# A four-batch decoder on one core: from two stages in flight to three, and experts in pairs

## The reference

```python
x = _layernorm(x + _L0_attn_ref(x, ...))            # linear attention, 16 heads, decay
x = _layernorm(x + _L0_xattn_ref(x, ctx_512, ...))  # similarity, norm, softmax
x = _layernorm(x + _L0_ffn_ref(x, ...))             # gated FFN of 688 with 8 low-rank experts
x = _layernorm(x + _L1_attn_ref(x, ...))            # Mamba: 512 channels, 16 states
x = _layernorm(x + _L1_xattn_ref(x, ctx, ctx))      # softmax attention, 32 query and 8 key heads
x = _layernorm(x + _L1_ffn_ref(x, ...))             # 16 experts of 176, top 4, and one of 704

# inside _L1_attn_ref, the state h of 512 x 16 per token:
h = h * dA_t + dBu_t
y = jnp.einsum('bdn,bn->bd', h, C_t)
```

## Time and profile before

| | us |
|---|---|
| median of 3 runs | 955.67 |
| lowest, highest | 949.19, 959.2 |
| the profiled execution, its own time | 949.86 |
| span of the profiled execution | 947.7 |
| PE, DVE, ACT, POOL busy in it | 828.1, 631.5, 369.4, 358.1 |

### The profile page before, as it was taken

The page is one execution under the profiler, slowest core; times in us unless marked ns, Lnnn a source line. Parts: engine busy times, 40 slices in busy tenths (PEclk is TensorE's granted clock), DMA queues, the critical chain, the costliest instruction groups (busy, mean ns, idle before and its releaser), DMA issues.

```text
span 947.7 us, 12835 instructions
## 1 busy us (share of the span) xinstructions
PE 828.1 (87%) x4575; PEld 629.4 (66%) x4600; DVE 631.5 (67%) x1322; ACT 369.4 (39%) x796; POOL 358.1 (38%) x390
## 2 busy tenths in 40 slices
PE   6897656989999898889999997889999898679997
PEld 5675445753788786753788786753788786426886
DVE  5242699785456999884456999895456999764333
ACT  5121555327325444326324444327324444253110
POOL 4302396121034875220034976121034976000322
PEclk9998757999999999998999999999999999999999
DMA  7202400011026340311016340311024340300442
GB/s 224 102 12 82 154 36 0 1 56 60 1 63 226 118 131 0 112 67 50 1 55 232 117 129 6 111 48 68 1 57 150 117 134 0 111 2 1 145 155 78
DMA packets 26930, 76.13 MB, mean 80 GB/s; under 512 B 3436, under 2 KB 5420, under 8 KB 26228
## 3 DMA queue, kind: packets, MB, share of 16 engines
q1 hardware_dynamic: 26612, 75.26, 24.2%
q10 hardware_dynamic: 256, 0.07, 0.0%
HBM read 74.13 MB, written 1.11 MB: 79 GB/s over the span
## 4 chain that ended last, share of the span: by engine, by line
PE 53%; DVE 24%; issue 10%; POOL 7%; ACT 4%; DMA 1%; ACTq 0%; DVEq 0%; POOLq 0%; SPq 0%
PE B L806 26%; PE F L806 19%; DVE arena L1477 7%; POOL arena L493 3%; PE B L1107 3%; DVE arena L1489 3%; DVE nmx L1549 2%; PE F L835 1%; DVE q_t L1610 1%; ACT big L773 1%; DVE arena L1310 1%; POOL arena L567 1%; PE F L817 1%; DVE q_t L1615 1%; POOL rs L473 1%
## 5 line engine op out<-in xcount | busy, mean ns | idle before, releaser
L806 PE MATMUL B<-spare,mw 128*128 128x256 f32 x880 | 210.5, 383 | 6.3 <-DVE q_t L1615 5.1
L806 PEld LDWEIGHTS B<-spare,mw 128*128 128x128 f32 x880 | 164.6, 191 | 31.7 <-issue 8.5
L1477 DVE TENSOR_TENSOR_SCAN arena<-F,arena 128x512 f32<-128x512 f32 x128 | 148.8, 1206 | 1.6 <-ACT F L733 1.5
L584 POOL TENSOR_TENSOR spare<-q_t 128x256 f32<-128x256 f32 x112 | 80.7, 729 | 173.2 <-DVE q_t L1615 160.4
L493 POOL TENSOR_TENSOR arena<-du,arena 128x1024 f32<-128x1024 f32 x60 | 140.9, 2363 | 12.9 <-PE B L888 12.9
L733 ACT ACTIVATE F<-delta,a_neg 128x255 f32<-128x255 f32 x256 | 109.7, 467 | 58.2 <-DVE arena L1477 58.2
L806 PE MATMUL B<-mw,spare 128*128 128x256 f32 x448 | 117.6, 388 | 0.0
L795 ACT ACTIVATE q_t<-B 128x256 f32<-128x256 f32 x112 | 41.9, 380 | 149.9 <-PE B L806 149.8
L806 PEld LDWEIGHTS B<-mw,spare 128*128 128x128 f32 x448 | 86.5, 195 | 14.1 <-issue 1.6
L773 ACT ACTIVATE big<-B 128x512 f32<-128x512 f32 x128 | 69.4, 594 | 51.1 <-PE B L806 38.5
L1610 DVE SCALAR_TENSOR_TENSOR q_t<-q_t,B 128x256 f32<-128x256 f32 x112 | 46.6, 416 | 57.3 <-ACT q_t L795 57.0
(11 more groups left out here) (246 smaller groups left out, 1323.8 us busy)
## 6 DMA issues: line engine op xcount, KB each, us to landing
mw<-in_w_moe SPq DMA_DIRECT2D x112, 384.0 KB, 3.1
room<-in_w_f SPq DMA_DIRECT2D x4, 2544.0 KB, 9.2
arena<-b_out SPq DMA_DIRECT2D x32, 256.0 KB, 5.3
room<-in_w_l SPq DMA_DIRECT2D x4, 768.0 KB, 6.9
w_m<-in_w_m SPq DMA_DIRECT2D x1, 2112.0 KB
room<-in_w_l SPq DMA_DIRECT2D x4, 512.0 KB, 5.0
x_t<-in_x_t SPq DMA_DIRECT2D x4, 256.0 KB, 3.7
x_tok<-in_x_tok SPq DMA_DIRECT2D x4, 256.0 KB, 6.6
```

What stands on the lines that cost most here:

```text
L584: g.tensor_tensor(hid1[0:r, m % HID_RING, :], hraw[0:r, m % 3, :], crs[0:r, int(m >= MTE), :], ALU.mult)\
L806: return t_.matmul(dst, lhsT, rhs, start=start, stop=stop, skip_group_check=True)
L1477: v.tensor_tensor_scan(h, F[i][:, :], h, 0.0, ALU.mult, ALU.add)\
```

## The change

It does four things.

**Three stages.** The front is cut behind `m1` into `FRONT_A` (attention, similarity, FFN) and `FRONT_B` (Mamba). `plan(engine)` writes: front half A of batch 0 alone; A of batch 1 with B of batch 0 put between its phases (`FILL`); twice an iteration of A of batch b+1, B of batch b and the back of batch b-1 (`LATER[0]`, `LATER[1]`); B of batch 3 with the back of batch 2 (`LATER[2]`); the back of batch 3. Inside an iteration `m2` and `m3` now stand between the last phases of the FFN of the next batch.

**Places.** Batch 1's half A runs on the banks K and in a second working area. That area, `late`, is the same memory that the backs use for expert weights, queries and probabilities, so back 0 waits for `x3` of batch 1. For batches 0 and 3 (`alone`) the factors of the scan go to an SBUF tile `factors` in place of F[0] and F[1], and F[1] takes the sum that lay in K[2]. Two copies of `xa` and `xp` exist. The keys of the next back are prepared by POOL in phase `br1` of the back before.

**Batch 0's scan** has the same form as the others: halves are added on POOL, and all multiplications by C are on DVE.

**Experts in pairs.** Two units share a gate bank and an up bank: one tanh, two DVE operations and one POOL operation of 128 x 512 in place of two each of 128 x 256. The matmuls are the same.

```diff
+FRONT_A = ["load", "qkv"] + PAIRS + ["oa", "ob", "xa", "xb", "xc", "xd", "fa1", "fa2", "fa3"] + FFN_G + ["fd1", "fd2", "fd3", "m1"]
+FRONT_B = ["m2", "m3", "m4", "m5", "d1", "d2", "d3", "d4"] + STEPS + ["u1", "u2"]
+FRONT = FRONT_A[:-3] + ["m2", "fd2", "fd3", "m3", "m1"] + FRONT_B[2:]
...
+def plan(engine):
+
+    out = [("F", ph, 0) for ph in FRONT_A]
+    out += merged(FILL[engine], [("F", ph, 1) for ph in FRONT_A], [("F", ph, 0) for ph in FRONT_B])
+    back = iter([("B", ph, b) for b in range(B) for ph in (BACK if b < B - 1 else BACK_LAST)])
+    parts = [[("F", ph, b + 1 if ph in FRONT_A else b) for ph in FRONT] for b in range(1, B - 1)]
+    parts.append([("F", ph, B - 1) for ph in FRONT_B])
+    for part, after in zip(parts, LATER[engine]):
+        for item in part:
+            out += [item] + [next(back) for _ in range(after.get(item[1], 0))]
+    return out + list(back)
...
+           {"m2": 1, "m3": 1, "m4": 1, "d1": 3, "d2": 9, "s0": 1, "s1": 10, "s2": 2, "s3": 1, "s4": 2, "s5": 1,
+            "s7": 2, "s8": 1, "s9": 1, "s10": 1, "s11": 2, "s12": 1, "s14": 4, "s15": 2, "u1": 26, "u2": 71}],
...
+        late = sb("late", [P, MW_RING * 3 * D + 2 * 2048 + (KT + HID_RING) * S + 2 * TT * D])
...
+        places = [Place(late if b == 1 else arena, K if b == 1 else F, xt1 if b == 1 else xt, xb1 if b == 1 else xb,
+                        xa2[b % 2], xp2[b % 2]) for b in range(B)]
...
+        def pair_banks(b, p):
+
+            return F[0:2] if b == B - 1 and p % 2 else K[0:2]
...
+        def y_bank(b, dp):
+
+            return (F[1] if alone(b) else K[2]) if dp else F[3]
+
+        def factor(b, i):
+
+            return factors[:, i, :] if alone(b) else F[i][:, :]
...
+        def alone(b):
+            return b in (0, B - 1)
...
-                    r = P if m < MT1 - 1 else HALF
-                    g.tensor_tensor(hid1[0:r, m % HID_RING, :], hraw[0:r, m % 3, :], crs[0:r, int(m >= MTE), :],
-                                    ALU.mult)\
-                        .then_inc(gb.step(f"hid{m}"), 1)
+                    s = 2 * p % HID_RING
+                    g.tensor_tensor(hid1[:, s:s + 2, :], pair_ring(p).rearrange("p (u t) -> p u t", u=2),
+                                    crs[:, int(2 * p >= MTE), :].unsqueeze(1).to_broadcast([P, 2, S]), ALU.mult)\
+                        .then_inc(gb.step(f"hid{p}"), 1)
...
-                    for u in range(2 if m < MT1 - 1 else 1):
+                    p, u = divmod(BE.index(ph), 2)
+                    lag = pair_lag(b)
+                    if p >= lag:
+                        pe.wait_ge(*db.at(f"gu{p - lag}" if u else f"st{p - lag}", b))
+                    for j in range(2 if 2 * p + 1 < MT1 - 1 or u == 0 else 1):
+                        m = 2 * p + j
...
+                            last = mm(pair_banks(b, p)[u][:, j * S:j * S + S], mw[:, slot, c:c + P], x5t[:, k, :],
+                                      k == 0, k == KT - 1)
```

More of the change, by code:

```diff
@@ L77, with merged @@
-AFTER_PE = {"load": 2, "qkv": 1, "at1": 1, "at2": 2, "at3": 1, "at4": 2, "at5": 1, "at6": 2, "at7": 3, "oa": 2, "ob":
[3 rows of a table removed]
-AFTER_DVE = {"load": 2, "at0": 1, "at1": 1, "at2": 2, "at3": 1, "at4": 2, "at5": 1, "at6": 3, "at7": 2, "oa": 8, "xa":
[3 rows of a table removed]
+FILL = {
[7 rows of a table added]
+}
+LATER = {
[35 rows of a table added]
+}
 IDLE_FIRST = {"xa": 7, "fa1": 19}
 IDLE_LAST = {"bq3": 11, "br1": 9}
-def merged(after):
-    assert sum(after.values()) == len(BACK)
-    back, out = iter(BACK), []
-    for ph in FRONT:
-        out += [("F", ph)] + [("B", next(back)) for _ in range(after.get(ph, 0))]
-    return out
+def merged(after, first, second):
+    assert sum(after.values()) == len(second)
+    rest, out = iter(second), []
+    for item in first:
+        out += [item] + [next(rest) for _ in range(after.get(item[1], 0))]
+    return out
@@ L438, in _ @@
             sp.dma_start(wr1[:, :, :], ins["wr1"]).then_inc(weights_in, 16)
+            load_context(0)
             idle = Steps(None, None, 0)
-            run(front, back, idle, idle, ORDER)
+            run(front, back, idle, idle, plan("ACT"))
             sp.wait_ge(out_done, 16 * B)
@@ L587, in back @@
                 if ph == "bout":
                     rsqrt(rsb[:, :], veb[:, :], db.at("ve_ln6", b), gb, "rs_ln6")
-            run(front, back, gf, gb, ORDER_POOL)
+            run(front, back, gf, gb, plan("POOL"))
         @block.scalar
@@ L788, in back @@
                     copy(crs.rearrange("p m n -> p (m n)"), K[3][:, :], ab, "crs", scale=0.5)
-                if ph in BE:
-                    m = BE.index(ph)
-                    act.wait_ge(*pb.at(f"gu{m}", b))
-                    if m >= 3:
-                        act.wait_ge(*db.at(f"gu{m - 3}", b))
-                    r = P if m < MT1 - 1 else HALF
-                    a.activation(thg[0:r, m % 3, :], gate_bank(b, m)[0:r, 0:S], ACT.Tanh, scale=0.5)\
-                        .then_inc(ab.step(f"th{m}"), 1)
-            run(front, back, af, ab, ORDER)
+                if ph in BE and BE.index(ph) % 2 == 0:
+                    p = BE.index(ph) // 2
+                    act.wait_ge(*pb.at(f"g{p}", b))
+                    if p >= PAIR_RING:
+                        act.wait_ge(*gb.at(f"hid{p - PAIR_RING}", b))
+                    a.activation(pair_ring(p), pair_banks(b, p)[0][:, :], ACT.Tanh, scale=0.5)\
+                        .then_inc(ab.step(f"th{p}"), 1)
+            run(front, back, af, ab, plan("ACT"))
         @block.tensor
@@ L877, in sum_states @@
                     pe.wait_ge(*af.at("delta0", b))
[L878 removed]
+                if n == 0 and not alone(b):
                     pe.wait_ge(*db.at("x4_read", b - 1))
                 if n < NSTEP - 1:
[L881 to L882 removed]
+                    pe.wait_ge(*(gf.at(f"half{n}", b) if in_halves(n) else df.at(f"hc{n}", b)))
+                parts = 1 if in_halves(n) else 2
                 if n < NTURN:
@@ L1463, in front @@
                     dve.wait_ge(*af.at("delta1", b))
-                    for bank in F[0:2]:
-                        v.memset(two(bank)[:, :, 0:1], 0.0).then_inc(df.step("first"), 1)
+                    for i in range(2):
+                        v.memset(two(factor(b, i))[:, :, 0:1], 0.0).then_inc(df.step("first"), 1)
                     step_input(b, 1)
@@ L1621, in back @@
                     db.mark("y")
-            run(front, back, df, db, ORDER_DVE)
+            run(front, back, df, db, plan("DVE"))
     return {n: s.number for n, s in steps.items()}
```

488 lines of the change are left out of this document (244 added, 244 removed), and 46 rows, old and new, of tables (AFTER_DVE, AFTER_PE, FILL, LATER).

## The result

| | before | changed |
|---|---|---|
| median, us | 953.15 (4 runs) | 1011.27 (4 runs, 1009.04 to 1014.58) |
| span of the profiled execution | 947.7 | 1010.8 |
| mean granted clock of PE | 0.957 | 0.918 |

The changed kernel takes 1.0597 times as long, 95% interval 1.0557 to 1.0637: 58 us slower by the medians. The forecast was 982 in a range of 955 to 1000, so the sign was right and the size was not.

A forecast was written before the change was run, and what follows sets the result against it. It took PE matmuls to nearly fill the iterations and DVE's scan to bound batch 0's Mamba. Start +49, iterations -6, last Mamba -20, clock +2, back 3 +1 made +26: 955.67 + 26 = 982 us, range 955 to 1000.

The forecast's parts named there:

- now 16 x 3.57 = 57.1: Batch 0's scan on DVE: sixteen steps of 3.57 us, 57.1 where it took 51.9, so +5.2; last Mamba also counts 57.1.
- The start: Front half A of batch 1 beside half B of batch 0, up to x4 of batch 0: +49 us, bounds +42 to +58.
- The first scan: Batch 0's first scan on DVE, after batch 1's attention and batch 0's convolution: at 143.5 us where before at 112.07, +31.4.
- The last Mamba: Half B of batch 3 beside back 2: 192 us where before 212.1, so -20, plus 2 for a lower clock.
- the eight table loads: ACT during batch 0's scan: eight loads of 1.3 us, 10.4 in all, mostly hidden; +4 taken, bounds 0 and 10.4.
- Iterations: The two middle stages (one A, one B, one back): -3 us each, -6 in all, bounds -12 and +6 each.
- as much room as before: Pair banks in the iterations: the gate bank frees after tanh and one DVE operation, with 3.5 us of matmuls between.
- Back 3: Batch 3's back alone: the last chain of its pairs gets longer at doubled width, +1 us.
- The last Mamba's order: Batch 3's scan beside back 2's attention, experts behind it: said to decide, two pieces end to end, 192 us in sum.
- The fast one: Rival: stages hide as meant, start +42, iterations -24, last stage -32; -14 in sum, 942 us; chance 0.11.
- the even one: Rival: start and last stage at their kind ends, +42 and -27, iterations 203 to 208; 953 to 963 us; chance 0.15.
- The start is worse: Rival: table loads fully on DVE +6, gate units delaying the scan +6, iterations gaining nothing +6; +44, 1000 us; chance 0.13.

## Why the prediction was wrong

**The step that failed** is one line of the start, "now 16 x 3.57 = 57.1", and the same 57.1 in the last Mamba's sum. It took the scan's duration from rows in which one input is in PSUM and used it for an instruction with both inputs in SBUF. The change names the new place (`factors`), and the prediction doesn't weigh it, either as a cost or as a bound. Measured: 22.7 and 21.6 us too little, since a scan stood still while POOL read SBUF. Moving one of the two factor banks made the kernel 28.7 shorter, and a short POOL operation with the factors left where they were made it 30.6 shorter.

**With that term put right the sums hold.** The start: +69.2 less 22.7 is +46.5, forecast +49 (+43 in the two other executions of this start). From the first scan to x4 it took 103.1, forecast 81.5: 21.6 more, which is that term. The first scan was forecast at 143.5 and came at 141.8; the rows are these:

```profile
123.16 5.26 DVE L1528 SCALAR_TENSOR_TENSOR arena<-F,vec,arena 128x255 f32<-128x255 f32 x12
...
139.20 1.30 DVE L1590 TENSOR_TENSOR du<-delta,u 128x512 f32<-128x512 f32 x2
...
141.76 2.17 DVE L1562 TENSOR_TENSOR_SCAN arena<-factors,arena 128x512 f32<-128x512 f32 x1 [1.25 <-ACT factors L812]
```

The last Mamba: 211.2 less 21.6 is 189.6, forecast 192, or 194 with the clock, with the experts in one piece behind the scan as read from the lists of order. That these sums met is for the total only: the eight table loads were entered with 4 of 10.4 us and no run took them alone.

**Iterations.** -5.8 each in place of -3, inside the bounds. The sign was right; the reason isn't shown. Pairs, one of the two causes that I named, cost 6 to 9 us an iteration in the kernel before with its own tables, and "as much room as before" was wrong there: PE came to wait 7.8 us for POOL's product. The gain may belong to the split of the stages, to the tables made with it, or to pairs with those tables; which of them, no run here tells.

**Back 3** was +6.5 in place of +1. The pairs are 3.6 of it, by the stretch of experts, which the run with pairs alone shows. The other 2.9 lie in its attention, from the mark to the fifth norm's statistics: 51.9 us before at a granted clock of 1.00, 53.2 with pairs alone at 0.97, 53.1 with one factor in PSUM at 0.94, 54.8 in the changed kernel at 0.81. The time follows the clock there, but no run sets the clock by itself; I had entered it for the last Mamba alone.

**The last Mamba's order** was called what decides. By the runs it was worth 7 us of the stage's 211 and some 1.4 of the kernel's time, the place of the factors 22. The prediction had 12 between the two orders (192, and 180 with experts within the scan); the role that it gave to the order belonged to the factors.

**The rivals.** The fast one and the even one needed the stages to hide what was DVE's, and didn't come near. "The start is worse" ended at 1000 by table loads and crossings; the time went past it by another mechanism, which was in no rival, and so the range ended too low. Nor did a full PE hide it: with SBUF factors everywhere it was paid nearly in full under a PE that had been 95% busy.

## What to carry to other kernels

When a change moves an operand, ask first whether the duration in the old rows still holds for its new place: here the DVE scans whose inputs both came to lie in SBUF ran in turn with POOL's operations on SBUF, and took 1.90 us in the mean in place of 1.21. Freeing PSUM banks by putting a scan's factors in SBUF cost 22 to 27 us for 32 scans; keeping one of two in PSUM took back 10 to 14 in each of two stages.

A stage whose PE is 95% busy did not cover a longer DVE step, with the steps' own matmuls in PE's list: some 26 us more of scan made 23 to 26 us more of stage.

A gain in one stage is counted only together with the next: of the 7 us that the other order took off the last Mamba, 5.6 came back in back 3.

Fewer, wider instructions can lower the busy time of the engine that runs them and lengthen the chain to the engine that waits for them: with pairs in the kernel before DVE was busy 3 us less in each iteration, and the iteration took 6 to 9 us more. Read the change at the waiter.

## What the runs showed of the hardware

The wait between DVE and POOL is not only for two SBUF inputs. The timelines show it at many places, though no run sets POOL's operation there by itself. In the run with the short chains moved ahead, the write of batch 1's second norm, a `tensor_scalar` with one tensor input, took 4.77 us for its two instructions, where it takes 0.73 elsewhere. In DVE's timeline:

```profile
154.53 4.77 DVE L1371 TENSOR_SCALAR xb<-xp,mv,rs 128x256 f32<-128x256 f32 x2 [0.81 <-POOL rs L559]
```

and in POOL's three inputs of the scan, back to back:

```profile
154.46 7.05 POOL L579 TENSOR_TENSOR arena<-du,arena 128x1024 f32<-128x1024 f32 x3
```

The same page and section of the Trainium skill names `tensor_scalar` among the instructions that can take the shared port; the rows agree, in that the two lasted as long as POOL's first two operations (154.46 to about 159.2). Elsewhere too the two last as long as what POOL runs beside them: 3.69 us from 165.51 on, beside two operations from 165.45 to 169.05, in the run with the scan beside the attention; 1.67 from 350.08 on, beside one from 350.02 to 351.28, in the changed kernel.

Both sides pay: with all factors in SBUF POOL was busy 105.9 and 108.3 us in the two iterations, and 84.2 and 84.7 in the changed kernel, for the same instructions (busy from start to end, waits inside an instruction counted).
